# Selection matmuls of a scan moved to the two halves of the array, with a new order of work

## The reference, cut to what matters

```python
def step(h, inp):
    dt_t, B_t, C_t, x_t = inp
    dA = jnp.exp(dt_t[..., None] * A)
    dBx = dt_t[..., None] * B_t[:, None, :] * x_t[..., None]
    h = dA * h + dBx
    y = jnp.einsum('bdn,bn->bd', h, C_t)
    return (h, y)
```

## Time and profile before

| | |
|---|---|
| three runs | 2100.76, 2107.02, 2113.20 us; median 2107.02 us |
| profiled execution: span, first to last instruction | 2098.0 us |
| profiled execution: its own total | not recorded; the span is 2.8 us under the fastest run and 9.0 us under the median |
| TensorE busy | 1751.1 us, 83% of the span |
| VectorE busy | 1350.6 us, 64% |
| GpSimd busy | 920.8 us, 44% |
| ScalarE busy | 661.1 us, 32% |

### The profile page before, as it was taken

One profiled execution on the slowest core, in us unless ns is written; L12 is line 12 of the kernel. 1 busy time (PEld: TensorE's weight loads), 2 busy tenths in 40 slices (PEclk: granted clock), 3 DMA queues, 4 the chain that ended last, 5 costly groups with the idle time before them and its releaser, 6 DMA issues.

```text
span 2098.0 us, 17739 instructions
## 1 busy us (share of the span) xinstructions
PE 1751.1 (83%) x6373; PEld 1001.5 (48%) x6373; DVE 1350.6 (64%) x1543; ACT 661.1 (32%) x1005; POOL 920.8 (44%) x689
## 2 busy tenths in 40 slices
PE   2025677668999988999989979999989699999988
PEld 1012222224654644665545535655646266665753
DVE  2397999966488966567989855579799410002355
ACT  1003232224235324333344334334343332223230
POOL 4678604777333337764843475565634000000000
PEclk7557787789999999999999989999999899999588
DMA  8454203333321133333311342433312012220000
GB/s 184 109 121 124 80 0 106 94 89 95 86 53 41 48 83 90 101 93 101 90 43 46 80 117 63 103 89 87 86 31 61 0 30 61 61 61 0 1 0 20
DMA packets 174927, 148.44 MB, mean 71 GB/s; under 512 B 137972, under 2 KB 138360, under 8 KB 174840
## 3 DMA queue, kind: packets, MB, share of 16 engines
q1 hardware_dynamic: 147192, 71.78, 14.1%
q0 software_dynamic: 27648, 75.53, 12.8%
HBM read 132.01 MB, written 15.24 MB: 70 GB/s over the span
## 4 chain that ended last, share of the span: by engine, by line
PE 58%; DVE 15%; ACT 3%; issue 3%; DMA 0%; DVEq 0%; ACTq 0%; SPq 0%
PE ps L872 41%; PE ps L875 12%; DVE tiles L1471 3%; DVE tiles L1480 2%; PE ps L1095 2%; DVE tiles L1463 2%; DVE slot L1414 1%; DVE tiles L1354 1%; ACT tiles L685 1%; ACT tiles L689 1%; PE ps L953 1%; DVE normal L1358 0%; PE ps L1028 0%; DVE sda L1500 0%; ACT tiles L691 0%
## 5 line engine op out<-in xcount | busy, mean ns | idle before, releaser
L630 POOL DMA_INDIRECT slot<-corners,index x576 | 695.6, 1208 | 375.4 <-issue 167.9
L872 PE MATMUL ps<-toep,tiles 128*128 128x512 f32 (+3 forms) x2048 | 589.2, 437 | 1.3 <-DVE tiles L1440 0.6
L872 PEld LDWEIGHTS ps<-toep,tiles 128*128 128x128 f32 x2048 | 369.6, 191 | 232.6 <-issue 140.6
L646 POOL TENSOR_TENSOR tiles<-tiles 128x1024 f32<-128x1024 f32 x90 | 217.1, 2412 | 302.4 <-DVE tiles L1471 297.5
L771 ACT COPY tiles<-ps 128x512 f32<-128x512 f32 x256 | 149.4, 584 | 462.6 <-PE ps L872 462.6
L875 PE MATMUL ps<-tiles,mring 128*128 128x128 f32 (+2 forms) x1024 | 246.2, 384 | 0.0
L1471 DVE TENSOR_TENSOR_SCAN tiles<-tiles 128x1024 f32<-128x1024 f32 x96 | 223.5, 2328 | 11.7 <-DVE tiles L1480 1.0
L756 ACT ACTIVATE tiles<-tiles,negA 128x1024 f32<-128x1024 f32 x128 | 146.6, 1148 | 215.7 <-DVE tiles L1471 196.2
L875 PEld LDWEIGHTS ps<-tiles,mring 128*128 128x128 f32 x1024 | 168.6, 193 | 78.4 <-issue 68.1
L872 PE MATMUL ps<-tiles 128*128 128x64 f32 (+5 forms) x770 | 177.0, 377 | 23.2 <-ACT tiles L787 11.5
L872 PE MATMUL ps<-tiles,sel 96*128 96x512 bf16 x512 | 149.6, 406 | 53.0 <-DVE tiles L1471 30.0
(11 more groups left out here) (236 smaller groups left out, 1984.3 us busy)
## 6 DMA issues: line engine op xcount, KB each, us to landing
toep<-in_phi_pad_dram SPq DMA_DIRECT2D x64, 513.0 KB, 4.0
mring<-mixing SPq DMA_DIRECT2D x128, 128.0 KB, 4.5
slot<-corners,index POOLq DMA_INDIRECT x576, 2.8
corners<-turned SPq DMA_DIRECT2D x128, 64.0 KB, 1.9
...
```

Of the source, the lines that this page charges most:

```text
L630: g.indirect_dma_start(out=slots[number % 3][:, k, :, :].rearrange("p a c -> p (a c)"), out_offset=None, in_=tables[h], in_offset=bass.Ind ...
L646: g.tensor_tensor(f(Y[h]), f(Y[h]), f(HC[n % 2]), ALU.add).then_inc(*ysum.up())
L872: return t.matmul(o, w, r, start=start, stop=stop)
```

## The change

The rows of B and C get halves of their own. `wxbc` has 128 columns: three copies of B's 16 columns at 0 to 47, three of C's at 64 to 111, zeros elsewhere; six small loads fill it where three did. `copy_rows` and `split_rows` work on 128 rows, and the subtraction of the parts is done by multiplying with a column of -1 and 0 (`less`). `sel` is 128 rows by 16 matrices, used for B and C alike. A spread matmul has 48 rows (K = 48): B on rows 0 to 47, C on rows 64 to 111. In pairs 1 to 3 a new unit "both rows" puts out C of a state and B of the next in turn, half tile by half tile, after the waits of both; the first B and the last C of each 16 states stay single, and so do all of pair 0. `TURNS` is replaced for all engines; of it the diff below keeps SP, POOL and the first and last lines of PE and DVE.

```diff
--- before.py
+++ after.py
@@ -65,7 +65,10 @@
     base[:, :, :, 1, :] = lin[tok // W].T[:, None, :, None]
     rank = np.broadcast_to(np.arange(EXPERTS, 0, -1), (P, EXPERTS))
     pick = (r[:, None] % 32 == np.arange(32)[None, :]) * 1.0
-    parts = [ident, mean_of(2), mean_of(16), mean_of(64), mask, base.reshape(P, -1), rank, pick]
+    part = r % 64 // N_STATE
+    state = ((r[:, None] % N_STATE == np.arange(N_STATE)[None, :]) & (part[:, None] < 3)) * 1.0
+    less = np.stack([(part < 2) * -1.0, (part < 1) * -1.0], 1)
+    parts = [ident, mean_of(2), mean_of(16), mean_of(64), mask, base.reshape(P, -1), rank, pick, state, less]
     return np.ascontiguousarray(np.concatenate(parts, 1).astype(np.float32))
 
 
@@ -198,7 +201,9 @@
                     if s == N_STATE:
                         dve += [("finish y", j, 0)]
                     continue
-                pe += [("b rows", j, s), ("c rows", j, s)]
+                if s % N_STATE == 0:
+                    pe += [("b rows", j, s)]
+                pe += [("both rows", j, s)] if s % N_STATE < N_STATE - 1 else [("c rows", j, s)]
                 pool += [("sum", j, s)]
                 dve += [("scan", j, s)]
                 if s % N_STATE < N_STATE - 1:
@@ -252,43 +257,43 @@
 CHUNKS = [(m, b, min(b + 4, m % BLK + 1)) for m in range(GROUPS) for b in range(0, m % BLK + 1, 4)]
 TURNS = {
     "SP": """
-        A9 C2 A3 C14 A2 C6 D A C10 A2 C7 D C25 E D""",
+        A9 C2 A3 C12 A2 C9 D A C11 A2 C5 D C25 D E""",
     "POOL": """
-        A288 B32 A121 B A3 B A B A B A6 B A4 B A4 B A4 B25 A124 B A2 B4 A10 B A4 B A4 B25""",
+        A288 B26 A5 B A2 B A B A2 B A4 B A6 B A115 B2 A3 B A3 B A3 B28 A144 B32""",
...
     "PE": """
-        A21 H A3 H7 B2 A3 B6 A B6 A3 B3 H B A B6 A2 B8 A B6 A3 B2 H B H2 B H B2 H B3 H2 A B3 A4 B2 A B10 A B6 A2 B6 A B6 A2 B A B5
...
-        D C6 D2 C6 D2 C6 D C6 D2 C8 D C D3 C D3 E3 D E2 D2 E2 D E2 D E D2 E2 D E D E2 D E D E2 D E3 D E2 D E3 D E2 D E3 D E2 D E3
-        D E2 D E D E2 D E D E2 D E3 D E3 D E5 D E8 D2 E D2 E3 D E D2 E D3 E D6 E D7 E D6 E33 D4""",
+        A21 H A3 H7 A B A2 B A B A2 B A B2 H B3 A B5 A2 B4 A B6 A B2 A B A B5 H2 B3 H2 B A B3 H2 B2 H A2 B A2 B2 A B13 A B6 A2 B6 A
...
+        C6 D C6 D C6 D C6 D C6 D C6 D C6 D C6 D C6 D C6 D C3 D2 C5 D C D2 C D3 E3 D2 E2 D E2 D E2 D E D2 E2 D E D E2 D E D2 E2 D2 E2
+        D E D E2 D E3 D E2 D E5 D E3 D E5 D E4 D2 E D3 E D E D2 E2 D2 E D E2 D E2 D2 E3 D2 E2 D2 E3 D2 E D2 E3 D2 E D3 E D5 E D E35""",
     "DVE": """
-        A45 H3 A3 H B6 A3 B6 A3 B3 A B2 A3 B6 A3 B7 A3 B6 A3 B3 A2 B6 H B H B A B H A H B5 A6 B8 A3 B6 A3 B7 A3 B6 A3 B4 A B A3 B7
...
-        D2 A D H D2 H D2 B17 A B6 A7 B A3 B6 A3 B5 A B9 H2 B2 H2 B47 C B2 C B2 C B C5 D2 C D2 C D C D2 C D2 C D9 C D C D3 C D2 E2
-        D E D E3 D E D E4 D E D E4 D E4 D E D E D E3 D E D E D E2 D E D E D E D E D E D3 E D E D2 E D3 E D2 E17 D2""",
+        A46 H A3 H A2 H2 A B A B A B4 A2 B A B A B2 A B A B2 A B A B2 A B A B2 A B A B2 A B7 A B A B7 A B H A B2 H B H B2 H B A B2 A
...
+        A D2 A D A3 D A D A4 D A2 D2 A2 D13 A B22 H B3 H B6 H B3 H B62 C B C B C4 D2 C2 D4 C D2 C D C D C D2 C D10 C D C D2 C D E2 D
+        E D E3 D E D E3 D E2 D E D E D E2 D E D E2 D E2 D E2 D E D2 E D E D2 E2 D E D E D E D2 E D E D2 E D3 E21""",
...
@@ -316,16 +321,18 @@
         base = cst[:, 5 * P:5 * P + 96]
         rank = cst[:, 5 * P + 96:5 * P + 104]
         pick = cst[:, 5 * P + 104:5 * P + 136]
+        state = cst[:, 5 * P + 136:5 * P + 136 + N_STATE]
+        less = [cst[:, 5 * P + 136 + N_STATE + n:5 * P + 137 + N_STATE + n] for n in range(2)]
         woff = sb("woff", [P, 3, 96])
         wmain = sb("wmain", [P, KTILES, 2, P])
         win = sb("win", [P, 3, P])
         wxdt = sb("wxdt", [P, DT_RANK])
-        wxbc = sb("wxbc", [P, 96])
+        wxbc = sb("wxbc", [P, P])
         wdt = sb("wdt", [DT_RANK, P])
         wxdtT = sb("wxdtT", [DT_RANK, P])
         wstep = sb("wstep", [P, P])
         wout = sb("wout", [P, 2, P])
-        sel = sb("sel", [96, 32, P], BF16)
+        sel = sb("sel", [P, N_STATE, P], BF16)
         negA = sb("negA", [P, N_STATE])
         wqkv2 = sb("wqkv2", [P, 3, P])
         wqkv3 = sb("wqkv3", [P, 3, P])
@@ -382,7 +389,8 @@
 
 
         ps = [ctx.enter_context(nc.psum_tensor(f"ps{n}", [P, L], F32)) for n in range(4)]
-        bcs = [F[0:96, BCS, HALF * h:HALF * h + HALF].bitcast(BF16) for h in range(2)]
+        bcs = [F[:, BCS, HALF * h:HALF * h + HALF].bitcast(BF16) for h in range(2)]
+        b_part, c_part = slice(0, 3 * N_STATE), slice(C, C + 3 * N_STATE)
         ring = [F[:, RING + n, :].rearrange("p (a t) -> p a t", a=2) for n in range(2)]
         sums = ps[0]
         ones, diag = F[:, 14, 0:P], F[:, 14, P:3 * P]
@@ -557,7 +565,9 @@
                 load(cols[:, 1:3], conv_w)
                 load(wxdt[:], W_x[:, 0:DT_RANK])
                 for q in range(3):
-                    load(wxbc[:, 32 * q:32 * q + 32], W_x[:, DT_RANK:])
+                    for n in range(2):
+                        load(wxbc[:, C * n + N_STATE * q:C * n + N_STATE * q + N_STATE],
+                             W_x[:, DT_RANK + N_STATE * n:DT_RANK + N_STATE * n + N_STATE])
                 load(wdt[:], W_dt)
                 load(negA[:], A_log)
                 load(brouter[:], bcast_row(router_b))
@@ -651,7 +661,7 @@
                 if unit == "sum":
                     add_product(j, m)
 
-            for tile in (wmain, win, wout, wqkv2, wqkv3, wrouter, wexp, bexp, mar, mring[0], mring[1]):
+            for tile in (wxbc, wmain, win, wout, wqkv2, wqkv3, wrouter, wexp, bexp, mar, mring[0], mring[1]):
                 g.memset(tile[:], 0.0)
             for n in range(2):
                 last = g.memset(normal[n][:, 0:2], 0.0)
@@ -725,7 +735,7 @@
 
             def copy_rows(j, h, q):
                 act.wait_ge(*rows_ps.at(j, 2 * h + q + 1))
-                a.copy(bcs[h][:, HALF * q:HALF * q + HALF], bank(("rows", j, 2 * h + q))[0:96, :]).then_inc(*bc_hi.up())
+                a.copy(bcs[h][:, HALF * q:HALF * q + HALF], bank(("rows", j, 2 * h + q))).then_inc(*bc_hi.up())
 
             def soft(j, h, q):
 
@@ -961,13 +971,13 @@
 
             def state_rows(j, h, q):
                 pe.wait_ge(*xc_ok.at(j, 2 * h + q + 1))
-                mm(take_bank(("rows", j, 2 * h + q))[0:96, :], wxbc[:], F[:, XC[h], HALF * q:HALF * q + HALF]).then_inc(*rows_ps.up())
+                mm(take_bank(("rows", j, 2 * h + q)), wxbc[:], F[:, XC[h], HALF * q:HALF * q + HALF]).then_inc(*rows_ps.up())
 
             def step_size(j, h, q):
                 pe.wait_ge(*xc_ok.at(j, 2 * h + q + 1))
                 mm(take_bank(("step", j, 2 * h + q)), wstep[:], F[:, XC[h], HALF * q:HALF * q + HALF]).then_inc(*step_ps.up())
 
-            def b_rows(j, s):
+            def wait_for_b(j, s):
                 h, n = s // N_STATE, s % N_STATE
                 if s == 0 and j >= 2:
                     pe.wait_ge(*place(j - 2).out_ok.at(j - 2, 1))
@@ -977,13 +987,40 @@
                 read = scan_ok if in_place(j) or s == 0 else bin_ok
                 if some(read.at(j, s)):
                     pe.wait_ge(*read.at(j, s))
-                wide(ps[2], sel[:, n, :], bcs[h]).then_inc(*b_ps.up())
+
+            def wait_for_c(j, s):
+                if some(hc_ok.at(j, s)):
+                    pe.wait_ge(*hc_ok.at(j, s))
+
+            def spread_b(h, n, q):
+                c = slice(HALF * q, HALF * q + HALF)
+                return mm(ps[2][:, c], sel[b_part, n, :], bcs[h][b_part, c])
+
+            def spread_c(h, n, q):
+                c = slice(HALF * q, HALF * q + HALF)
+                return mm(ps[3][:, c], sel[c_part, n, :], bcs[h][c_part, c])
+
+            def b_rows(j, s):
+                h, n = s // N_STATE, s % N_STATE
+                wait_for_b(j, s)
+                spread_b(h, n, 0)
+                spread_b(h, n, 1).then_inc(*b_ps.up())
 
             def c_rows(j, s):
                 h, n = s // N_STATE, s % N_STATE
-                if some(hc_ok.at(j, s)):
-                    pe.wait_ge(*hc_ok.at(j, s))
-                wide(ps[3], sel[:, N_STATE + n, :], bcs[h]).then_inc(*c_ps.up())
+                wait_for_c(j, s)
+                spread_c(h, n, 0)
+                spread_c(h, n, 1).then_inc(*c_ps.up())
+
+            def both_rows(j, s):
+
+                h, n = s // N_STATE, s % N_STATE
+                wait_for_c(j, s)
+                wait_for_b(j, s + 1)
+                spread_c(h, n, 0)
+                spread_b(h, n + 1, 0)
+                spread_c(h, n, 1).then_inc(*c_ps.up())
+                spread_b(h, n + 1, 1).then_inc(*b_ps.up())
 
             def sum_states(j, s):
                 h, n = s // N_STATE, s % N_STATE
@@ -1183,6 +1220,8 @@
                     b_rows(j, m)
                 if unit == "c rows":
                     c_rows(j, m)
+                if unit == "both rows":
+                    both_rows(j, m)
                 if unit == "sum":
                     sum_states(j, m)
```

(11 more changed lines are left out.)

50 lines of the change are left out of this document (25 added, 25 removed).

## The result

The changed kernel is slower: median 2134.29 us (4 runs, 2128.47 to 2137.87) against 2109.28 us (4 runs of the kernel before on the same chip): ratio 1.0124, 95% interval 1.0092 to 1.0156. The prediction was 2095, range 2070 to 2124.

A forecast was written before the change was run, and what follows sets the result against it. VectorE was taken to bound pair 0's scan, TensorE slightly the later scans (4.91 against 4.68 us a state). Terms -11.6 + 0.9 - 2 = -12.7 us from 2107.0 gave 2094, say 2095 us; range 2070 to 2124.

The forecast's parts named there:

- Turns made anew: New order on all engines: same large shape, -2 us at the end, 0 elsewhere with 15 us either side.
- The prediction's last sign of being wrong: Whole run: time going with stretches where neither engine is full would point to the new turns; no size given.
- Overlap and price of a half: Spread matmuls, pairs 1 to 3: joint unit 0.45 us, saving 0.42; lone half unit costs 0.28 us (0.09 + 0.09 + 0.10).
- What that is worth (-11.6): Pairs 1 to 3: 37.8 us saved less 25.5 lost, 12.3 us off TensorE, at 0.93 to 0.96 11.6 us.
- nothing to be won: Rival, chance 0.17: VectorE's 4.68 us round rules, savings only lengthen its waits, setup's 0.9 us stays: 2107 to 2108.
- Joint wait at nothing: "Both rows" units, pairs 1 to 3: waiting for product and B bank costs nothing, as VectorE's 2.3 us scan covers 0.55.
- Pair 0 at nothing: Pair 0's scan: 42 lone half units cost TensorE 11.8 us, hidden in its 83 us free, so 0.
- the rival's mechanism: Pair 0's scan, chance 0.17: TensorE becomes the bound, B rows come after VectorE has finished; 24 us added, 2119 or more.
- The sign named for it: Pair 0: VectorE's waits for B rows appearing there would show the forecast wrong; no size given.
- Setup +0.9: Setup and row splitting: extra loads +1.4 us, shorter selection cast -1.1, split steps +0.6 in pair 0; sum +0.9.
- Tail -2: End of the kernel: pair 2 is stored before pair 3's experts begin; gain at most 3.2 us, taken as 2.
- the halves don't overlap: Rival, chance 0.05: bf16 matmuls on the two halves don't run side by side, 25.5 us paid for nothing: 2132.

The follow-up runs named there:

- e2: The kernel before with the new turns on all engines, each joint unit taken apart into C and B units, no halves: 2133.94 us, ratio 1.0113.
- x1: The changed kernel with the old order of TensorE, VectorE and ScalarE up to the end of pair 0's scan, new order afterwards: 2129.12 us, ratio 1.0119.
- e1: The changed kernel with the turns of the kernel before on all engines, 88 joint units kept: 2072.77 us, ratio 0.9825.
- w3: The kernel before plus two small matmuls, results never read, in each of 24 attention query groups: 2080.07 us, ratio 0.9866.
- w2: e4 plus two small matmuls, results never read, in each of 24 attention query groups: 2074.56 us, ratio 0.9843.
- e4: e1 with single B and C units reading all 128 rows, only the joint units using halves: 2095.88 us, ratio 0.9930.
- q1: e1 plus two small matmuls, results never read, in each of 24 attention query groups: 2082.28 us, ratio 0.9884.

## Why the prediction was wrong, step by step

**The failing step is "Turns made anew".** I read the new lists for their large shape and their end, took 0 elsewhere, "and keep 15 us to either side". The order alone costs 26 us of the median (e2), and 46.6 us at the end of pair 3's scan in the profiled execution. I bounded it by TensorE's idle time in the scans (12.5 and 15.4 us), which is the room for a better order and no bound for a worse one. What I should have read was VectorE's list against GpSimd's pace: 9 gathers a group of 1.2 us and 0.30 us between them, one group in 13 to 14 us in this stretch with either order. Each sampling group that the new list puts ahead of a head step, a norm or a scan step holds these until its gather has landed. Counted that way, "first scan step of pair 1 behind group 13 instead of 9" is four groups of 13 us, less what was free; x1, whose pair 0 ends on time, begins pair 1 21 us later than e1. That holds for the part before 580 us; the cost of the new order behind it stays open. The prediction's last sign of being wrong, time that goes with stretches in which neither engine is full, was seen in pair 0's scan (88% and 72%). The Trainium skill's TensorE: Matmul & The Clock Gate, section "Architectural detail", calls ScalarE and VectorE strict FIFOs; the rows of 179.48 to 194.68 us show it of VectorE, a ready split step waiting 14.6 us behind an unready weigh.

**Overlap and price of a half: right.** 0.54 us a joint unit with its drain, 0.09 us ahead and 0.10 behind, as taken from the earlier trace rows. That TensorE's busy time fell by 15.3 us where I expected about 10 proves nothing, since e2, without halves, has 1729.9 us, still less; at the same clock the joint units take 15.1 us off it (w3 1727.1, w2 1712.0).

**What that is worth (-11.6): too much, right in sign.** I put 93 to 96% of it on the path. For the joint units alone the milestones give 6.5 us (e4 against before) and 3.8 us (w2 against w3) at the end of pair 3's scan. In both pairs of runs pair 1's scan is 3.8 to 3.9 us shorter; in e4 pair 2's is 0.5 shorter and pair 3's not at all, which fits the rival "nothing to be won": in the old order VectorE's round would set pairs 2 and 3. With the new order TensorE is the full engine of pair 3's scan (157.91 of 160 us); there the three scans of after are together 9.7 us shorter than e2's, and 7.7 us remain at the end of pair 3's. But this sets the second shortest of four executions of after against the longest of e2, and their medians are equal, so a gain there isn't shown.

**Joint wait at nothing: right** as far as the runs show, since the scans of pairs 2 and 3 are as long in e1 as before. **Pair 0 at nothing: wrong by 4 to 6 us.** The 83 free microseconds did not hide all of 33 lone places: 240.4 against 235.9 us (e1, e4), and 6.4 us between q1 and w2 at the end of pair 3's scan. It is the rival's mechanism at a fifth of its price: the B row does come after VectorE is done, by 1.0 us at most and 5.3 us in all, and VectorE stays the busier engine. The sign named for it was seen (4.7 us in pair 0 of the kernel after). In the other pairs the waits for B rows grew from 57.0 to 67.5 us, but e2 has 76.7 without halves.

**Setup +0.9: about nothing.** The loads cost what I said (six in 2.83 us) and the cast 1.22 us, but VectorE's wait for the last load is 30.4 us against the earlier trace rows 29.8 and ends 0.25 us earlier:

```profile
93.86 0.18 DVE L1311 TENSOR_SCALAR negA<-negA 128x16 f32<-128x16 f32 x1 [30.40 <-DMA brouter<-in_router_b_dram]
```

The split steps take 742 and 751 ns, as bounded by the earlier trace rows.

**Tail -2: -7.8 us** in the profiled runs, but the clock, of which the prediction says nothing there, can be all of it: the kernel before lost it for 55 us, the kernel after for 30, and half of the difference, as an estimate, is 12 us:

```profile
2015.00:2045.00 30.00, 23.95 (x68) 14.79 (x68) 15.82 (x45) 7.05 (x16) 0.00 (x0) 0.53 0.00 0
```

The time given for "the halves don't overlap", 2132, is near the result by accident; the timeline after shows the overlap.
